# A layer of state-space mixer and product-key experts on one core: first and last groups rearranged, the searches' steps on GpSimd, and the search weights' product in two halves

## What is computed

```python
x = x + layernorm(attn(layernorm(x)))        # attn(u) = u + mamba(rmsnorm(u))
x = x + layernorm(ffn(layernorm(x)))

def mamba(u):                                # 8 heads of 64, state 128, chunks of 128 tokens
    z, xbc, dt = split(u @ in_proj_w.T)      # 512, 2560, 8
    xh, B, C = split(silu(conv4(xbc)))       # causal convolution over 4 tokens
    scores = (C @ B.T) * decay * dt          # within a chunk
    y = scores @ xh + (C * exp(cum)) @ H_prev + D_skip * xh
    return rmsnorm(y * silu(z), gnorm_w) @ out_proj_w.T

def ffn(h):                                  # 4 retrieval heads, 2 x 64 keys, best 8
    sim = (h @ W_q.T) . keys                 # 2 sides x 4 heads x 64 keys
    s, i = top8(top8(sim_x) + top8(sim_y))   # expert number = 64 * ix + iy
    w = silu((h . down_embed[i]) * softmax(s))
    return w @ up_embed[i] + silu(h @ W_up.T) @ W_down.T
```

## Time and profile before

| | |
|---|---|
| median of three runs | 2789.25 us |
| profiled execution, its own time | 2791.39 us |
| its span, first to last instruction | 2789.70 us |
| mean granted clock of TensorE | 0.989 |
| busy: TensorE, its weight loads | 2641.5 us (95%), 2173.9 us (78%) |
| busy: VectorE, GpSimd, ScalarE | 2396.5 (86%), 2058.8 (74%), 1750.7 us (63%) |

### The profile page before, as it was taken

How to read it: one execution, slowest core, us unless ns; L and a number is a source line. 1 busy time by engine, 2 the same in 40 slices (tenths; PEclk the granted TensorE clock), 3 DMA queues, 4 the chain that set the end, 5 groups by cost and what they waited for, 6 DMA issues and landing times. The chain is left out here.

```text
span 2789.7 us, 49914 instructions
## 1 busy us (share of the span) xinstructions
PE 2641.5 (95%) x14624; PEld 2173.9 (78%) x14688; DVE 2396.5 (86%) x5638; ACT 1750.7 (63%) x3688; POOL 2058.8 (74%) x2880
## 2 busy tenths in 40 slices
PE   5999999999999999999999999999999999999985
PEld 4778877878877878877878877878877878877873
DVE  4588889988889988889988889988889888889885
ACT  4566666666666666666666666666666666666653
POOL 3367787877787877787877777877777877777866
PEclk9999999999999999999999999999999999999998
DMA  3000000000000000000000000000000000000000
GB/s 135 8 9 12 5 8 11 11 11 11 4 8 11 11 11 11 4 8 11 11 11 11 0 11 11 11 11 11 0 11 11 11 11 9 2 11 11 8 5 8
DMA packets 28182, 34.23 MB, mean 12 GB/s; under 512 B 2672, under 2 KB 27248, under 8 KB 27440
## 3 DMA queue, kind: packets, MB, share of 16 engines
q1 hardware_dynamic: 28144, 33.77, 3.7%
HBM read 25.37 MB, written 8.39 MB: 12 GB/s over the span
## 5 line engine op out<-in xcount | busy, mean ns | idle before, releaser
L1104 DVE SCALAR_TENSOR_TENSOR acc<-bank,cw,acc 128x253 f32<-128x253 f32 x1920 | 770.4, 470 | 120.8 <-ACT acc L783 120.2
L1434 PE MATMUL bank<-hT,w_in 128*128 128x256 f32 x2560 | 607.5, 383 | 40.0 <-DVE acc L1104 39.2
L620 POOL TENSOR_TENSOR Em<-ee 128x1024 f32<-128x1024 f32 x256 | 562.0, 2215 | 64.9 <-DVE yv L1145 53.6
L1434 PEld LDWEIGHTS bank<-hT,w_in 128*128 128x128 f32 x2560 | 481.1, 191 | 156.7 <-DVE acc L1104 54.0
L1266 DVE SCALAR_TENSOR_TENSOR Em<-Em,p 128x1024 f32<-128x1024 f32 x256 | 429.6, 1678 | 1.7 <-POOL Em L620 1.7
L917 ACT ACTIVATE Em<-Em,rden 128x1024 f32<-128x1024 f32 x256 | 293.0, 1145 | 113.6 <-DVE Em L1275 113.5
L635 POOL TENSOR_TENSOR W<-W,Em 128x1024 f32<-128x1024 f32 x128 | 330.6, 2583 | 8.5 <-ACT Em L917 0.3
L783 ACT ACTIVATE acc<-bank,cb,cw 128x253 f32<-128x253 f32 x640 | 323.5, 559 | 0.0
L1275 DVE TENSOR_TENSOR Em<-Em,products 128x1024 f32<-128x1024 f32 x256 | 310.7, 1214 | 4.6
L1604 PE MATMUL products<-w_de,h2T 128*128 128x512 f32 x512 | 239.0, 610 | 44.2 <-DVE Em L1275 44.1
L1619 PE MATMUL bank<-h2T,w_up 128*128 128x256 f32 x1024 | 242.2, 379 | 1.4 <-ACT sim L887 0.7
(11 more groups left out here) (199 smaller groups left out, 5342.3 us busy)
## 6 DMA issues: line engine op xcount, KB each, us to landing
x_in<-x_dram SPq DMA_DIRECT2D x32, 256.0 KB, 2.7
x_res<-x_dram SPq DMA_DIRECT2D x32, 256.0 KB, 2.7
out_dram<-f SPq DMA_DIRECT2D x32, 256.0 KB, 2.2
w_in<-in_wT_dram SPq DMA_DIRECT2D x1, 3080.0 KB, 12.3
w_up<-upT_dram SPq DMA_DIRECT2D x1, 1024.0 KB, 15.1
w_de<-down_eT_dram SPq DMA_DIRECT2D x1, 1024.0 KB, 17.1
w_down<-downT_dram SPq DMA_DIRECT2D x1, 1024.0 KB, 19.1
w_ue<-up_e_dram SPq DMA_DIRECT2D x1, 1024.0 KB, 21.2
```

What stands on the lines that cost most here:

```text
L620: nc.gpsimd.tensor_tensor(Em[:, k], bc(ee[:, k, 0:XD], 2, KEYS), bc(ee[:, k, XD:XD + KEYS], 1, XD), ALU.mult).then_inc(E_done.sem, 1)
L1104: ins = V.scalar_tensor_tensor(acc[:, r, a, TAPS - 1:], ps[:, a * TOK + k:(a + 1) * TOK - TAPS + 1 + k], cw[:, t, k:k + 1], acc[:, r, a, T ...
L1434: last = mm(ring[j % 2][:, a * TOK:(a + 1) * TOK], w_in[:, k, at:at + P], hT[:, k, :], start=k == 0, stop=k == DK - 1)
```

## The change

1. Loads and folding: `w_in` is loaded and folded in three parts (x, B and C, z); `w_out`'s fold and `skip` come later; the first convolution pairs wait for their part alone.
2. The search weights' product moves from ahead of group 0 into group 0, between z and pair 4; it goes into `fA`, each matmul split into two of 64 output partitions.
3. The four subtractions of `ffn_best` move from VectorE to GpSimd (`ffn_args`), for both chunks around the convolution's heads. GpSimd waits for `rden` ahead of `mixer_scale(g, 0)`; `weigh(e, 1, 0)` goes behind the root of y and loses its gate; `tail_keep` moves on ScalarE behind pairs 0 and 1 of the next group; on VectorE the mask of head 3 goes ahead of the store and of times 2.
4. The last two turns become one list, `ending(31, 30)`: the products of chunk 0 go to the banks `ring`, and TensorE adds the four heads itself (`ffn_sum`) while it transposes them.

The diff, cut to its core (the last piece is VectorE's `ending`):

```diff
+            sp.dma_start(cb[:], conv_b).then_inc(loaded_c, 16)
+            at = INNER + 4 * TOK
+            sp.dma_start(w_in[:, :, INNER:at], in_wT[:, :, INNER:at]).then_inc(loaded_x, 16)
+            sp.dma_start(w_in[:, :, at:], in_wT[:, :, at:]).then_inc(loaded_bc, 16)
+            sp.dma_start(w_in[:, :, 0:INNER], in_wT[:, :, 0:INNER]).then_inc(loaded_z, 16)
+            sp.dma_start(hid[0:64, :, :], wq).then_inc(loaded_s, 16)
...
+            def ffn_args(e, c):
+                pool.wait_ge(best_done.sem, best_done.at(e, c * RH + RH - 1))
+                if c == 0 and later(e):
+                    pool.wait_ge(E_done.sem, E_done.at(e - 1, CH * RH - 1))
+                rows = ee[:, c * RH:(c + 1) * RH]
+                nc.gpsimd.tensor_tensor(rows[:, :, XD:XD + KEYS], sim[:, c, 1], bc(s8[:, c, 1, :, 0], 2, KEYS),
+                                        ALU.subtract).then_inc(own_pool, own.one())
...
                 if a:
                     mixer_cum(g)
                     mixer_parts(g)
+                if b:
+                    ffn_args(e, 0)
+                if a:
                     mixer_head(g)
+                if b:
+                    ffn_args(e, 1)
...
+                if b:
+                    pool.wait_ge(rden_done.sem, rden_done.at(e))
                 if a:
                     mixer_scale(g, 0)
...
             def ffn_best(e, c):
...
-                V.tensor_tensor(rows[:, :, 0:XD], sim[:, c, 0, :, 0:XD], bc(s8[:, c, 0, :, 0], 2, XD),
-                                ALU.subtract).then_inc(own_dve, own.one())
...
+            def search_weights():
+                pe.wait_ge(loaded_s, 16 * 2)
+                for k in range(DK):
+                    for s in range(2 * RH):
+                        at = k * 2 * RH * KEYS + s * KEYS
+                        for half in range(2):
+                            last = mm(fA[64 * half:64 * half + 64, at:at + KEYS],
+                                      hid[0:64, s, k * P + 64 * half:k * P + 64 * half + 64],
+                                      WT[0:64, 0:4, :].rearrange("p a (b k) -> p (a b) k", k=KEYS)[:, s, :],
+                                      start=True, stop=True)
+                    last.then_inc(simw_ps, 1)
...
+            def ffn_sum(e, c, before, added):
+                for q in range(2):
+                    pe.wait_ge(WT_sb.sem, WT_sb.at(*before[q]))
+                for h in range(RH):
+                    flat = Em[:, c * RH + h].rearrange("p a b -> p (a b)")
+                    pe.wait_ge(Zs_done.sem, Zs_done.at(e, c * RH + h))
+                    if h == 1:
+                        pe.wait_ge(last_added, added)
+                    for i in range(ET):
+                        last = mm(pairb[i // 4][:, i % 4 * P:(i % 4 + 1) * P], flat[:, i * P:(i + 1) * P], ident[:],
+                                  start=h == 0 and i % 4 == 0, stop=h == RH - 1 and i % 4 == 3)
...
+            def ending(e, f):
+                ffn_last(f, 1)
+                ffn_mask(f, 1, 0)
+                tail_residual(e)
+                ffn_times(f, 1, 0)
+                for h in (1, 2):
+                    ffn_mask(f, 1, h)
+                    ffn_times(f, 1, h)
+                ffn_best(e, 0)
+                ffn_best(e, 1)
...
```

More of the change, by code:

```diff
@@ L617, in weigh @@
                         pool.wait_ge(rden_done.sem, rden_done.at(e))
-                    if later(e):
+                    if later(e) and not summed:
                         pool.wait_ge(W_part.sem, W_part.at(e - 1, c * (RH - 1) + max(h - 1, 0)))
@@ L954, in do_group @@
                 if c:
+                    tail_keep(f)
                     ffn_experts(f, 0, 3)
@@ L969, in do_group @@
                     mixer_z(g, 1)
+                if a and not later(g):
+                    search_weights()
                 if b:
@@ L1037, in do_group @@
                     ffn_experts(e, 0, 2)
-                    tail_keep(e)
             mixer_norm(0, None)
@@ L1302, in do_group @@
                 conv(1)
+                if a and not later(g):
+                    fold(loaded_z, 0, INNER)
                 if c:
@@ L1315, in do_group @@
                 conv(7, 8, 9)
+                if a and not later(g):
+                    fold_out()
                 if b:
@@ L1362, in _ @@
             mixer_stats(0)
-            dve.wait_ge(loaded_out, 16)
-            for k in range(INNER // P):
-                V.tensor_scalar(w_out[:, k, :], w_out[:, k, :], gw[:, k:k + 1], None, ALU.mult)\
-                    .then_inc(own_dve, own.one())
-            dve.wait_ge(own_dve, own.n)
-            dve.sem_inc(folded, 1)
+            dve.wait_ge(loaded_c, 16 * 6)
+            fold(loaded_x, INNER, INNER + 4 * TOK)
+            fold(loaded_bc, INNER + 4 * TOK, PROJ)
             do_group(0, None, None, 1)
@@ L1596, in ffn_sim, with ffn_A @@
                 last.then_inc(sim_ps.sem, 1)
-            def ffn_A(e, c):
-                if c or later(e):
+            def ffn_A(e, c, two=None):
+                if two is None and (c or later(e)):
                     pe.wait_ge(Z_done.sem, Z_done.at(e, c * RH - 1))
@@ L1663, in pairs @@
                             mixer_pair(g, j)
+                if a and not later(g):
+                    pe.wait_ge(folded, 2)
                 pairs(0, 1)
+                if a and not later(g):
+                    pe.wait_ge(folded, 4)
                 if a:
@@ L1677, in do_group @@
                     ffn_down(f, 1)
+                if a and not later(g):
+                    pe.wait_ge(folded, 6)
                 if a:
```

234 lines of the change are left out of this document (157 added, 77 removed).

## The result

The changed kernel takes 2713.68 us (median of 4 runs, 2712.61 to 2715.71) against 2788.80 us for the kernel before (now four runs): ratio 0.9731, 95% interval 0.9714 to 0.9748. I had forecast 2749 us, 2724 to 2779.

What follows compares the result with a forecast made beforehand. TensorE, busy 95% of the span, was taken as the bound, with two short stalls for VectorE a period. Steady groups -31, start -10.6, end +1 gave -40.6 us, so 2749 us by the median, range 2724 to 2779 (8 in 10).

Steps and rivals of the forecast that it cites:

- The second stall: Experts' first product after a group's end waits 0.72 us for VectorE; forecast 0 us gained, bounds -0.72 and +0.2 a period.
- rival (a): Steady groups: both stalls go or the period tightens further, 30 x 0.72 less, 2727 us; chance 0.14.
- The first stall: Convolution pair 9 waits 1.03 us for VectorE; moving the search steps to GpSimd removes it, 30 x 1.03 = -31 us.
- rival (b): Pair 9's stall is replaced: GpSimd's steps make ScalarE and Ldec 1 us late; 2779 us, chance 0.15.
- The start: Loads, folding and group 0: stream 16.7 us earlier, search product +7.0, clock -0.9; -10.6 us, bounds -16 and -3.
- rival (e): Start: search weights' product takes half, 3.5 us less, since the weights' columns set the pace; 2745.5 us, chance 0.25.
- The end: Last groups: 4.6 us won at the exponentials, then TensorE bound with longer head sums; +1 us in all.
- the fall at w_ue: Ending: after a 3.4 us gap of TensorE the clock may fall and add up to 5 us; not in the sum.
- Rival (c): Group's end: Em takes the port ahead of VectorE's store, products stall 2.9 us instead of 0.72; +66, 2815 us, chance 0.06.

Runs made afterwards that it cites:

- e2: Changed kernel with GpSimd's Em of head 0 of chunk 1 ahead of the root of y again, behind the wait for y: 2737.89 us.
- e3: Changed kernel with VectorE's mask of head 3 behind the store again (mask 2, times 2, store, mask 3): 2797.59 us.
- e4: Kernel before with only the searches' exponent steps moved to GpSimd, without the wait for rden: 2749.38 us.
- e8: Changed kernel with the search weights' product in two passes, all matmuls of one output half and then the other: 2716.17 us.
- e7: Changed kernel with the search weights' product unsplit, 16 matmuls of 128 output partitions: 2718.67 us.
- e14: Changed kernel with exponent steps on VectorE, Em ahead of the root of y, mask 3 behind the store, and the old ending; new start kept: 2777.37 us.
- e9: Changed kernel with one swap in the ending, ScalarE's exponentials ahead of the first up copy: 2708.10 us.
- e11: Changed kernel, ending swapped: exponentials ahead of up copy, w_down ahead of products and transposes, residual ahead of mask: 2701.92 us.
- e13: Changed kernel with exponent steps on VectorE, Em ahead of the root of y, mask 3 behind the store; new start and ending kept: 2785.83 us.
- e5: Changed kernel with both edits of the group's end undone, Em ahead of the root of y and mask 3 behind the store: 2742.17 us.
- e6: Changed kernel with the old ending, two calls of the common program in place of the new list: 2706.72 us.
- e1: Changed kernel with the searches' exponent steps back from GpSimd on VectorE: 2819.43 us, 1.0109 of the kernel before.

## Why the prediction was wrong, step by step

By the profiled executions the change brought -75.7 us and I had -40.6.

**The second stall: the step that failed.** I stepped through the group's end with "the one that waits gets the port next", which put the root between the masks, came to 1439.5 against 1439.4 and took 0 us, with -0.72 a period as the bound "if both masks go through before a root gets in". That bound is what happens: the square sum reached GpSimd's root at 1383.52, 1.2 us into the masks, the next mask followed without a gap, and the root's power waited. So the masks took 2.48 us and the products' wait went: 0.88 x 30 = -26 us, in my sum as nothing. It is rival (a), which I gave 0.14. What I had against it, that the disturbance only moves to the neighbours, is true in each edit by itself (e2, e3), and false for both: the neighbours it moves to are GpSimd's own root, for which nobody waits here, and a times step that reads PSUM. I priced the edits one by one where only the pair counts.

**The first stall: right mechanism, wrong size.** The steps on VectorE made pair 9 late, and GpSimd's take their place at no cost (e4). But I charged the idle time in brackets, 1.03 us, where the period lost 1.30: 30 x 0.27 = 8 us missed. Together the two stalls are 65 us where I had 31. In group 1, which I had left out, the moved steps bring about 2 us more (e4). My range for 8 in 10 ended at 2724, the case of both stalls at their bracket price (2727); with 1.30 and 0.88 in their place the same sum gives 2749 - 30 x 0.27 - 30 x 0.88 = 2714.5, the time measured (in part by luck, since start and end were off by 5 to 6 us each, in opposite directions). GpSimd's steps, 0.63 + 0.30 + 0.44 us a chunk against my 1.6, were near enough, and rival (b) did not come about: with GpSimd's steps alone (e4) the period fell by all of the 1.3 us, so heads and exponentials cost TensorE nothing.

**The start: the gain counted too small.** First conv at 12.59 us (forecast 11.9, before 28.59): -16.0. The search product took 2.08 us where I put 7.0, and even rival (e) said 3.5: it had the rule on the weights' columns, worth half (e8), but not the overlap of the halves. Group 0 as a whole gave 2.2 us back and not 6.1, though in the profiles of the kernels with this start it took 46.6 to 48.5 us (e7 aside), so that figure holds to 2 us. Of the 3.0 us that went in group 1 only 1.2 are the start's (e14, 77.2 us instead of 78.4); the 0.94 at pair 9 (a wait of 1.19 us became 0.25) is the moved steps' (e4 has it, e14 has 1.05). So the start is about -15 in this trace against -10.6; alone it is worth -11.2 by medians (e14) and -14.0 by the two profiled executions, that of before being 2.8 us above its median.

**The end: +6.6 instead of +1.** The stepped order was right: exponentials, WT and the TensorE-bound rest came in the order that I gave. But I took the search's matmuls and w_ue at full clock. They ran at the lower level behind their waits: 1.9 + 1.7 us for the searches, 2.9 us for w_ue. I had named the fall at w_ue, "up to 5", and left it out of the sum. e9 to e11 show that the waits could be filled.

**Rival (c)**, Em ahead of the store, did not come about in the change, but it exists: e3 shows it in the old order of masks, with a wait of 1.34 us (I had said 2.9) and the lower clock behind it, at +84 us against the change.

Ledger by medians, a chain in which each kernel is compared with the next, so that it must add up to the whole: start -11.2 (e14 against before), new ending +8.5 (e13 against e14), the exponents' steps -43.7 (e5 against e13), the two edits of the group's end -28.5 (the change against e5): -74.9. The ending is +7.0 by e6, and e13's runs spread over 7.6 us. The steps are -38.4 by e4 and -106 by e1: what a part is worth depends on the kernel around it.

## What to carry to other kernels

Price a stall from start to start of the rows around it, with and without it, not by the idle time in brackets; here 1.03 us idle cost 1.30. When two engines share a port and an edit moves one instruction, step through all orders of arrival, and where one of them removes the stall and another doubles it, give both real chances: edits that are harmful alone can be the gain together. In an ending, fill the waits of TensorE with work that is ready: here they cost their own time and put the matmuls behind them at the lower level, and three swaps took 11.8 us off.

## What the runs showed of the hardware

- A stall can cost more than its length, but its length alone doesn't say whether. In the steady groups, behind 0.72 and 1.03 to 1.09 us the next matmuls kept the granted clock of 1.00 (3.70 us for the products). Behind 1.34 us (e3) the products took 5.40 us in 18 of 24 groups and 3.70 in the others. Behind 1.96 us (e1) pair 9 took from 1.99 to 3.68 us. In the ending of e11 the search behind 2.74 us stayed at full clock (1.98 us), in that of the change the one behind 0.94 us didn't (3.60 us).
- So the same edit, the exponents' steps, was worth 43.7 us where the products' stall stood (e5 against e13) and 106 us where it was gone (e1).
- Matmul instructions with 64 x 64 weights in fp32: 0.059 us an instruction one half after the other (e8), 0.032 with the halves in turn; with weights of 64 rows and 128 columns 0.112 (e7, its first 26).
- A power of two elements a partition on GpSimd takes 0.71 us alone and 1.59 us behind VectorE's mask: VectorE can hold GpSimd up as well as GpSimd VectorE (0.21 us became 1.27 and 2.19).
